# Last batch: residual prepared ahead, output in two halves, one state product on VectorE, and a new order of all steps

## The reference

```python
xn = layernorm(x)
s  = attention(xn)                    # q k^T / 128, own token masked, softmax, times v
g  = silu(top-2-of-8 experts(xn))     # 128 -> 256 -> 128, every expert is computed
x  = x + s * g
xn = layernorm(x)
s  = mamba(xn)                        # rms norm, in-projection, conv, scan, out-projection, + xn
g  = silu(top-1-of-8 experts(xn))     # 128 -> 512 -> 128, tokens sorted to their expert
x  = x + s * g
```

## Time and profile before

| | us |
|---|---|
| median of three runs | 978.26 |
| lowest, highest | 975.25, 983.37 |
| the profiled execution | 977.57 |
| its span, first to last instruction | 975.8 |
| busy: PE, DVE, ACT, POOL | 854.6, 777.3, 632.0, 592.7 |

### The profile page before, as it was taken

One profiled execution on the slowest core, in us unless ns is written; L12 is line 12 of the kernel. 1 busy time (PEld: TensorE's weight loads), 2 busy tenths in 40 slices (PEclk: granted clock), 3 DMA queues, 4 the chain that ended last, 5 costly groups with the idle time before them and its releaser, 6 DMA issues.

```text
span 975.8 us, 15806 instructions
## 1 busy us (share of the span) xinstructions
PE 854.6 (88%) x4624; PEld 583.0 (60%) x4624; DVE 777.3 (80%) x1479; ACT 632.0 (65%) x1379; POOL 592.7 (61%) x556
## 2 busy tenths in 40 slices
PE   5987898999799978999799979999799967785995
PEld 2773475775467746775567746775567735552662
DVE  3234537899988998799888998799888998877995
ACT  3524735868577775878477766878487765665661
POOL 0010202758856595858866694858766696869675
PEclk9987799999999998999899998999899997877999
DMA  7200103223322432224212332224213332333451
GB/s 265 88 1 13 33 12 98 85 76 123 99 71 75 109 120 85 84 87 132 95 55 87 107 120 75 84 88 133 93 57 106 95 109 98 117 99 95 134 146 52
DMA packets 79429, 90.28 MB, mean 93 GB/s; under 512 B 8450, under 2 KB 49906, under 8 KB 78834
## 3 DMA queue, kind: packets, MB, share of 16 engines
q1 hardware_dynamic: 77298, 85.07, 27.9%
q0 software_dynamic: 2048, 4.20, 1.5%
HBM read 52.96 MB, written 13.04 MB: 68 GB/s over the span
## 4 chain that ended last, share of the span: by engine, by line
PE 53%; POOL 17%; DVE 15%; issue 10%; ACT 4%; SPq 1%; DMA 0%; DVEq 0%; POOLq 0%
PE work L825 9%; PE work L831 7%; POOL st L1474 7%; PE work L856 7%; DVE st L1304 6%; PE work L866 5%; PE yacc L890 5%; POOL y L1481 4%; PE work L754 3%; PE work L775 3%; POOL fe L1461 3%; POOL du L1435 2%; PE work L745 2%; PE work L798 2%; ACT prob L946 1%
## 5 line engine op out<-in xcount | busy, mean ns | idle before, releaser
L1474 POOL TENSOR_TENSOR st<-st,Cs 128x512 f32<-128x512 f32 x249 | 315.9, 1281 | 184.4 <-DVE st L1304 182.2
L946 ACT ACTIVATE dA<-delta,Aneg 128x512 f32<-128x512 f32 x256 | 176.0, 722 | 9.6 <-DVE st L1304 9.1
L1304 DVE TENSOR_TENSOR_SCAN st<-dA,dbu 128x512 f32<-128x512 f32 x128 | 154.8, 1210 | 13.4 <-ACT dA L946 9.2
L890 PE MATMUL yacc<-st,w_ident 128*128 128x512 f32 x256 | 141.3, 637 | 27.2 <-POOL st L1474 27.2
L1304 DVE TENSOR_TENSOR_SCAN st<-dA,b_row 128x512 f32<-128x512 f32 x123 | 148.7, 1209 | 2.9 <-DVE acc L1194 1.5
L831 PEld LDWEIGHTS work<-w_w2a,hid 128*128 128x128 f32 x1024 | 121.5, 192 | 27.6 <-issue 13.0
L825 PE MATMUL work<-xnT,w_w1a 128*128 128x512 f32 x256 | 130.4, 600 | 5.9 <-ACT ys L946 3.8
L1481 POOL TENSOR_TENSOR y<-y,st 128x512 f32<-128x512 f32 x105 | 133.4, 1271 | 2.9
L946 ACT ACTIVATE hsT<-work,hs 128x128 f32<-128x128 f32 x352 | 100.6, 373 | 49.5 <-PE work L856 49.5
L831 PE MATMUL work<-w_w2a,hid 128*128 128x128 f32 x1024 | 124.9, 276 | 7.6 <-DVE delta L1278 7.6
L856 PE MATMUL work<-xsT,hs 128*128 128x128 f32 x704 | 106.6, 303 | 19.1 <-ACT xsT L946 17.9
(11 more groups left out here) (190 smaller groups left out, 1308.3 us busy)
## 6 DMA issues: line engine op xcount, KB each, us to landing
Cs<-c_dram SPq DMA_DIRECT2D x128, 256.0 KB, 3.6
hs<-w_w1f SPq DMA_DIRECT2D x88, 258.0 KB, 2.4
xs_in<-xs_dram SPq DMA_DIRECT2D x16, 256.0 KB, 2.8
ys_dram<-ys SPq DMA_DIRECT2D x16, 256.0 KB, 3.9
w_w1f<-in_w1f_dram SPq DMA_DIRECT2D x1, 2064.0 KB, 8.1
x_in<-in_x_dram SPq DMA_DIRECT2D x8, 256.0 KB, 3.3
w_w2f<-in_w2f_dram SPq DMA_DIRECT2D x1, 2048.0 KB, 12.4
kept_dram<-x_tok SPq DMA_DIRECT2D x8, 256.0 KB, 4.5
```

The lines of the kernel that those rows point to most:

```text
L890: mm(yacc[:], ident[:], state(s), start=False, stop=(n == NS - 1)).then_inc(sig["y_sum0"], 1)
L946: return nc.scalar.activation(out, in_, func, **k)
L1304: V.tensor_tensor_scan(state(s), dA[:, s % DECAYS], (dbu0, rows_bank(n, b))[h][:], 0.0, ALU.mult, ALU.add).then_inc(sig["scan"], 1)
L1474: G.tensor_tensor(state(s), state(s), Cs[:, b.of(NS, n) % C_BUFS], ALU.mult).then_inc(sig["P"], 1)
```

## The change

All values are computed as before. In the last batch:

- `xr` becomes `0.5 * xn * g + xr` before the out-projection is there: POOL makes `y1 = xn * g`, DVE the rest.
- The out-projection goes into two banks, the first two tiles of 128 tokens into one and the last two into the other, with a signal after each. DVE turns each half into the output with two instructions of half the size, and SP stores each half by itself.
- The C product of step 31 is on DVE behind the last scan and not on POOL.

The places, shifts and banks of nearly all steps are new numbers, in all batches. The core of the diff:

```diff
-                elif g == "C" and name == "out":
+                elif g == "C" and name == "out" and b.is_(NB - 1):
+                    for k in range(2):
+                        sp.wait_ge(sig["ot"], b.of(1, k + 1))
+                        sp.dma_start(out[b.n, 256 * k:256 * k + 256].rearrange("(i p) d -> p i d", p=128), ot[:, 2 * k:2 * k + 2]
+                                     ).then_inc(sig["out"], 16)
...
-                pe.wait_ge(sig["P"], b.of(STEPS, s + 1))
+                if n == NS - 1:
+                    pe.wait_ge(sig["P_last"], 1)
+                else:
+                    pe.wait_ge(sig["P"], b.of(STEPS, s + 1))
                 mm(work[SPARE][:], ident[:], state(s), start=(n == 0), stop=(n == NS - 1)).then_inc(sig["y_sum1"], 1)
...
                 for t in range(NT):
+                    if b.is_(NB - 1) and t == NT // 2:
+                        last.then_inc(ready[g], 1)
+                        w = other_bank(b)
...
+            def last_times_c(s, b):
+
+                r = b.of(NS, NS - 1)
+                dve.wait_ge(c_ld[r % C_BUFS], 16 * (r // C_BUFS + 1))
+                dve.wait_ge(sig["scan"], b.of(STEPS, s + 1))
+                V.tensor_tensor(state(s), state(s), Cs[:, r % C_BUFS], ALU.mult).then_inc(sig["P_last"], 1)
...
                     if b.is_(NB - 1):
-                        dve.wait_ge(sig["xr"], b.of(16, 16))
-                        V.tensor_tensor(ot[:], ot[:], xr[:], ALU.add).then_inc(sig["ot"], 1)
-                    dve.sem_inc(free_of("C", step, b), 1)
+                        dve.wait_ge(sig["rest"], 1)
+                        V.scalar_tensor_tensor(xr[:], y1t, 0.5, xr[:], ALU.mult, ALU.add).then_inc(sig["opx"], 1)
+                        for k in range(2):
+                            half = slice(2 * k, 2 * k + 2)
+                            dve.wait_ge(ready["C"], READY["C", step, b.n] + k)
+                            r = tiles((bank("C", step, b), other_bank(b))[k][:])[:, half]
+                            V.scalar_tensor_tensor(r, r, 0.5, g1[:, half], ALU.mult, ALU.mult).then_inc(sig["s1"], 1)
+                            dve.wait_ge(sig["opx"], b.of(1, 1))
+                            dve.wait_ge(sig["s1"], b.of(1, k + 1))
+                            V.tensor_tensor(ot[:, half], r, xr[:, half], ALU.add).then_inc(sig["ot"], 1)
...
+                elif g == "C" and name == "op" and b.is_(NB - 1):
+                    pool.wait_ge(sig["g1"], b.of(1, 1))
+                    pool.wait_ge(sig["xr"], b.of(16, 16))
+                    G.tensor_tensor(y1t, xn1_tok[:, b.n % 2], g1[:], ALU.mult).then_inc(sig["rest"], 1)
...
-    ("P", "pe", 0, -1.09268, 7, -2, -3, None),
+    ("P", "pe", 0, -1.00164, 7, 4, 2, None),
```

More of the change, by code:

```diff
@@ L325 @@
     ("A", 0): (
[4 rows of a table removed]
[4 rows of a table added]
     ),
     ("H", 0): (
-        -1.11411, -1.06978, -1.05742, -0.89565, -0.90279, -0.83828, -0.88733, -0.81603, -0.81528, -0.80089, -0.79422, -0.57863,
-        -0.79157, -0.74780, -0.77419, -0.79303, -0.73709, -0.72833, -0.62595, -0.89555, -0.69538, -0.77574, -0.66455, -0.53536,
-        -0.45046, -0.49154, -0.77058, -0.61446,
+        -1.06926, -1.11488, -1.07138, -0.90278, -1.02776, -0.90721, -0.93188, -0.88885, -0.88768, -0.83181, -0.80060, -0.62522,
+        -0.80029, -0.78513, -0.77066, -0.79205, -0.74524, -0.73956, -0.65961, -0.27137, -0.69281, -0.78227, -0.77960, -0.61707,
+        -0.61469, -0.77950, -0.70521, -0.74534,
     ),
     ("A", 1): (
[4 rows of a table removed]
[4 rows of a table added]
     ),
@@ L530, in build @@
         y1 = sb("y1", [128, T])
+        y1t = y1[:].rearrange("p (i d) -> p i d", i=NT)
         dA = sb("dA", [128, DECAYS, T])
@@ L595, in bank, with other_bank @@
             return work[bank_of(g, step, b.n)]
+        def other_bank(b):
+            return work[1 - bank_of("C", ("op", 0), b.n)]
         def free_of(g, step, b):
@@ L700, in _ @@
                 do(g, step, Batch(n))
-            sp.wait_ge(sig["out"], 16 * NB)
+            sp.wait_ge(sig["out"], 16 * NB + 16)
         @block.tensor
@@ L903, in project @@
                 bank_free(pe, g, step, b)
+                if b.is_(NB - 1):
+                    last = LAST_IN[1 - bank_of(g, step, b.n)]
+                    emptied(pe, *last[:2], Batch(last[2]))
                 pe.wait_ge(sig["yo"], b.of(1, 1))
+                w = bank(g, step, b)
                 for t in range(NT):
+                    if b.is_(NB - 1) and t == NT // 2:
+                        last.then_inc(ready[g], 1)
+                        w = other_bank(b)
                     for h in range(NH):
-                        last = mm(bank(g, step, b)[:, t * 128:(t + 1) * 128], du[:, par, h, t * 128:(t + 1) * 128],
+                        last = mm(w[:, t * 128:(t + 1) * 128], du[:, par, h, t * 128:(t + 1) * 128],
                                   W["woutT"][:, h * 128:(h + 1) * 128], start=(h == 0), stop=(h == NH - 1))
@@ L1319, in c_step @@
                 elif step[0] == "op":
-                    filled(dve, "C", step, b)
                     since(dve, sig["out"], b.of(16))
-                    r = tiles(bank("C", step, b)[:])
-                    V.tensor_tensor(r, r, xn1_tok[:, par], ALU.add).then_inc(sig["opx"], 1)
-                    dve.wait_ge(sig["opx"], b.of(1, 1))
                     dve.wait_ge(sig["g1"], b.of(1, 1))
-                    V.scalar_tensor_tensor(ot[:], r, 0.5, g1[:], ALU.mult, ALU.mult).then_inc(sig["s1"], 1)
-                    dve.wait_ge(sig["s1"], b.of(1, 1))
                     if b.is_(NB - 1):
-                        dve.wait_ge(sig["xr"], b.of(16, 16))
-                        V.tensor_tensor(ot[:], ot[:], xr[:], ALU.add).then_inc(sig["ot"], 1)
-                    dve.sem_inc(free_of("C", step, b), 1)
+                        dve.wait_ge(sig["rest"], 1)
[8 more added lines that the diff above has]
+                            V.tensor_tensor(ot[:, half], r, xr[:, half], ALU.add).then_inc(sig["ot"], 1)
+                    else:
+                        filled(dve, "C", step, b)
+                        r = tiles(bank("C", step, b)[:])
+                        V.tensor_tensor(r, r, xn1_tok[:, par], ALU.add).then_inc(sig["opx"], 1)
+                        dve.wait_ge(sig["opx"], b.of(1, 1))
+                        V.scalar_tensor_tensor(ot[:], r, 0.5, g1[:], ALU.mult, ALU.mult).then_inc(sig["s1"], 1)
+                        dve.wait_ge(sig["s1"], b.of(1, 1))
+                        dve.sem_inc(free_of("C", step, b), 1)
             def do(g, step, b):
@@ L1344, in do @@
                     scan(i, b)
+                    if b.is_(NB - 1) and i == STEPS - 1:
+                        last_times_c(i, b)
                 elif g == "C":
@@ L1490, in do @@
                     f_step(step, b)
-                elif g == "S" and name == "p":
+                elif g == "S" and name == "p" and not (b.is_(NB - 1) and i == STEPS - 1):
                     times_c(i, b)
@@ L1494, in do @@
                     add_state(i, b)
-                elif g == "C" and name == "op" and not b.is_(NB - 1):
+                elif g == "C" and name == "op" and b.is_(NB - 1):
+                    pool.wait_ge(sig["g1"], b.of(1, 1))
+                    pool.wait_ge(sig["xr"], b.of(16, 16))
+                    G.tensor_tensor(y1t, xn1_tok[:, b.n % 2], g1[:], ALU.mult).then_inc(sig["rest"], 1)
+                elif g == "C" and name == "op":
                     pool.wait_ge(sig["s1"], b.of(1, 1))
```

## The result

The changed kernel takes 983.18 us (median of 22 runs, 979.22 to 988.53), the kernel before 978.72 (22 runs beside it, 974.86 to 983.75). The ratio is 1.0051, with a 95% interval of 1.003 to 1.0072: slower by half a per cent. Forecast were 979.5, a range of 967 to 989, and 0.74 for "within 1%"; the measured median is 3.7 above the first. The profiled execution took 980.58, its span is 978.8 against 975.8. What follows counts span: 3.0 us are to be explained by it.

A forecast was written before the change was run, and what follows sets the result against it. Bound: a ring per period, POOL's queue from `pos` to `ft`, then PE's from h0 to `rk`. Terms +10.3 - 1.2 - 8.7 + 0.8 = +1.2 on 977.57 gave 978.8, or 979.5 by median; range 967 to 989.

The forecast's parts named there:

- Start, +10.3 -1.2: Start: beta products ahead of H.z0 cost 10.3 us; y0 and b1 moved out of PE's later full stretch give 1.2.
- The rival that they run at full clock: Start: beta products stay at full clock and take 7.0 us, z0 is 5.3 later, total 974.5; chance 0.15.
- Periods, -8.7: All periods: `ft` sooner gives 1.35 us in each of five, 1.9 in the sixth; bounds 0 and -16.
- the clock: 0.4: Behind each period's stall: PE's slow-clock stretch shrinks somewhat, giving 0.4 us a period.
- a clock of 1.00 behind the stall: Period's end: a granted clock of 1.00 behind PE's stall would show the forecast wrong.
- The period without A: Sixth period, where DVE leads: 1.4 us from DVE's wait for PE and 0.5 from its wait ahead of H.bc.
- worth only what DVE waits for PE there: Period without A: the sixth stall's gain is limited to DVE's wait of 1.48 us for PE, taken as 1.4.
- Tail, +0.8: Behind the last scan: C.y starts later and the residual chain takes 4.4 us; 0.8 us slower, bounds -0.6 and +1.8.
- The DVE product of step 31 lies in 5.67 us of idle time: Tail: DVE's product of step 31 costs nothing, at worst 0.7 us for a POOL step that it holds up.
- The start decides, slower: Start: all 64 products, z0 and x1T at half clock, +13.7 us; periods give only 0.95 each; total 984.3; chance 0.25.
- The periods win: Periods: the slow stretch shrinks by half or more, each period gives 2.9 us, total 971.1; chance 0.2.
- The tail does what its name says: Tail: the rest of the residual is made during the scans; gives 0.6 us, total 978.1; chance 0.05.

The follow-up runs named there:

- e1: The changed kernel with the beta products back in their old place, ahead of H.hT on PE: 973.04 us, ratio 0.9923 to the kernel before.
- e2: The kernel before with the beta products alone moved behind H.xi0 on PE: 993.91 us, ratio 1.0154 to the kernel before.
- e3: The changed kernel with `ft` late again, behind two other steps in POOL's queue: 999.92 us, ratio 1.0223 to the kernel before.
- e4: The kernel before with `ft` alone moved ahead of two other steps in POOL's queue: 976.58 us, ratio 0.9979 to the kernel before.
- e5: The changed kernel with the last batch's scan 31 written to PSUM, where DVE's C product reads it: 985.24 us in one execution.
- e6: The changed kernel with the last batch's `g` made ahead of C.y on DVE: 986.48 us in one execution.
- e8: The changed kernel with the edits of e1, e5 and e6, and a15 ahead of e15 on PE: 969.87 us, ratio 0.9924 to the kernel before.
- e10: The same program as e8, run a second time beside e9: 967.88 us, ratio 0.9908 to the kernel before.
- e9: The code of e8 with the order tables of e7: 969.47 us, ratio 0.9917 to the kernel before.
- e15: Not a run: a step of the kernel with work on PE and POOL, which DVE's C.y needs; no time of its own as a run.
- e7: e4 with y0 also moved ahead of a0 in PE's queue: 973.13 us, ratio 0.9938 to the kernel before.

## Why the prediction was right, and where not

The time lies in the range and within 1%, as forecast. By span the sum was +1.2 and +3.0 came. The terms were off by more, in both directions: the start 2.7 us dearer, the tail 1.7 dearer, the periods and the last scans 2.6 cheaper. That they nearly cancel is luck. (Of the rivals' times, 971.1 and 984.3 stand on the scale of the profiled execution and 974.5 and 978.1 on that of the median, 0.7 higher. "No gain in the periods" adds up to 991 and not 990.)

**Start, +10.3 -1.2.** The mechanism is as forecast: e1 and e2 each show it with one number moved. The size was too small: the products took 13.65 us, the upper bound of the forecast (13.5), where I took 12.0 for "a short spell at full". There was none: PE had idled 12.58 us before hT, hT and xi0 ran at half clock, and the clock stayed there. With z0's own 1.05 us more, that makes 12.8 of the 12.6 us. The row that I leaned on was the wrong neighbour: in the old place PE came into the products out of full work, at 1.00, in the new one out of rest, at 0.50. The first interval gave back 0.8 of the 1.2. That this comes from y0 and b1 is not shown: e2, which moves nothing there, gave back 1.45. The rival that they run at full clock, 0.15, fell: the rows have 0.50 while PE is busy 3.40 of 3.40 us. The rule of the Trainium skill, "TensorE: Matmul & The Clock Gate", Part 1, that the clock follows busy time, would have given 7.0 us; the windows disagree, and the measurement decides.

**Periods, -8.7.** Measured: -11.2 in the five, +0.4 in the sixth. `ft` sooner and ACT late next was the right reading: -2.3 from `pos` to h0 where 1.95 was forecast, ACT's F.silu with no idle time before it, and e3 and e4 show it with this one step moved. The mis-sized term is the clock: 0.4 was taken, with a bound of 3 if the spell went. From h0 to `pos` the steps moved in (0.8) and the wait for the copy (0.2) were to cost 1.0, less 0.4 for the clock; measured is 0.05 a period. So the clock, if all of it is the clock, gave 0.95. The trace of the kernel before bears this out: its h0 with 3.4 us of half clock takes 72.2 us to the next `pos`, the other four 73.4 on the mean. Had all five been like the first, they would sum to 361.0 us. The changed kernel has 366.0, 1.0 more a period, which is what the steps and the copy were to cost; and the kernel before has 365.8, so its clock cost 0.95 a period. The reason that I gave for a small term, PE's idle time bunching even more ahead of h0, was wrong in the trace: it lies in pieces of 1.19, 0.89 and 1.45 us with PE's steps between them. But the pieces don't settle the length of the half clock either. It is 3.4 and 6.8 us behind the same 2.8 in the kernel before, and 0 and 3.4 behind the same 1.3 to 1.5 in the changed kernel. What decides it stays open. One of the forecast's signs of being wrong, a clock of 1.00 behind the stall, is there in two periods of five, and another, a new wait of over half a us on PE that repeats, is the 0.76 above.

The -11.2 is also the good end of what this order does. From the second `pos` to the last scan it gains 11.3 us on the kernel before in its own trace, and 6.9, 9.2, 9.3, 8.2 and 12.0 in those of e1, e5, e6, e8 and e10, which have the same order there (but for a15 in the last two): 9.5 on the mean of the six. For that the forecast had 8.7.

The period without A was to give 1.9 and took 0.4. The 1.48 and 2.08 us of the earlier trace rows are gone, and DVE has new waits in their stead. Two of 0.42 and 0.41 us are for ACT, at 836.08 and 837.71; the other two in its timeline in the changed kernel:

```profile
852.53 0.19 DVE L1157 TENSOR_REDUCE am<-work 128x4 f32<-128x32 f32 x1 [1.06 <-PE work L790]
856.24 1.22 DVE L1323 TENSOR_TENSOR_SCAN st<-dA,dbu 128x512 f32<-128x512 f32 x1 [1.70 <-PE yacc L899]
```

Their sum is 3.6 us, what the old ones held. In this trace the step that fails is "worth only what DVE waits for PE there": a wait taken away in a queue that is moved as a whole is not yet time won. But in e1, e5 and e10, with the same order, the wait of 1.70 is 0.6 or less, and the period takes 92.8, 92.1 and 92.9 us for the 94.6 before: 1.7 to 2.4 less, as forecast. So the failure is this execution's, and the order does not force it.

**Tail, +0.8.** Measured +2.5, 2.1 to the last sum and 0.4 for the store. The 0.4 is not shown to be the split's: from the last sum to the end it is 2.6 us before, and with the store split it is 3.0 here and in e3 but 2.2 in e6, e8, e9 and e10. That half the size gives 0 isn't shown either: in the changed kernel's trace stores of 256 KB land after 2.6 us and those of 128 KB after 1.8 (medians), where the kernel before had 3.1 for 256 KB and for 32. The failing step is "The DVE product of step 31 lies in 5.67 us of idle time: nothing, and at worst 0.7". It took 5.17 us, and e15 then waited 0.42 for it at half clock. C.y's middle instruction starts 8.49 us after the last scan, 6.53 before: +1.96 where 0.75 was forecast. e5 takes the block away and leaves the 14.4 us, so the block is not the sole cause: PE's last four steps at half clock take as long. The clock alone is not the cause either: in e3, which keeps block and order, it is back at full 4.3 us behind the last scan, as early as before, and C.y's middle instruction still starts 8.15 us after that scan, 1.6 later than before. The longer half clock adds 0.3 to that here. With `g` ahead, the product from PSUM and a15 ahead of e15 (e8) 2.5 us go. e6 gives `g` 1.5 of them; how the rest divides between a15 and the product, no run tells apart. The chain behind C.y was right, 4.50 us for 4.4 forecast.

**The rivals.** "The start decides, slower" had 984.3 and named half clock for all 64 products, which is what happened; its other half, a period that gives only 0.95, did not. "The periods win" had the spell that shrinks by half, which happened as well. "The tail does what its name says" fell by e6. The number came out near the first of them because gains in the periods ran against it, as far as the second has them: not its 2.9 us a period, but 2.2.

## What to carry to other kernels

Filler work belongs where an engine has nothing to do, and a queue's order is to be read for what it uncovers: 64 tiny products, free in one gap, cost 10 to 15 us behind the next step. Before a stall is shortened, look at what its late engine's next step will wait for (e4 gave 1.8 us, one more move 3.4). A product moved to an idle VectorE beside a busy GpSimd was short here only with one of its inputs in PSUM. And one trace each is not enough: the same order gained 6.9 to 12.0 us in six of them.

## What the runs showed of the hardware

**VectorE behind GpSimd.** A tensor product on DVE with both inputs in SBUF took 5.17 us in the changed kernel and again in e1, e3 and e6, 0.69 with one input in PSUM (e5, e8). It began 0.3 us after POOL's first product and ended 0.56 us after POOL's fourth instruction in a row. A hint was in the trace of the kernel before, at 805.56: C.y's middle instruction, two inputs in SBUF, begins 0.07 us after a single product of POOL, takes 1.75 us and ends 0.56 after it. In the six other periods it takes 0.76. The Trainium skill, "SBUF — State Buffer", section "Who interferes with whom", has a VectorE instruction with two SBUF inputs contend with GpSimd's reads for a shared port, so that the one that comes second waits for the other's whole instruction. The trace agrees that it waits, but it waited for four instructions, not for one.

**The start varies, and so do the periods.** With the same order at the start, the first `pos` came at 109.9, 109.6, 112.8 and 116.8 us (changed kernel, e3, e5, e6), with the beta products back at 103.0, 95.5 and 100.3 (e1, e8, e10), and with the old order at 97.3, 97.3, 99.8 and 99.7 (before, e4, e7, e9). Windows of 80 to 95 us in e8 and e10, columns as in the earlier trace rows:

```profile
80.00:95.00 15.00, 9.77 (x48) 5.27 (x48) 8.43 (x25) 7.72 (x15) 0.00 (x0) 0.93 0.00 1
```
```profile
80.00:95.00 15.00, 13.54 (x32) 7.46 (x33) 5.68 (x14) 5.47 (x11) 0.00 (x0) 0.57 0.00 1
```

e8 and e10 are one program: 0.93 granted in the one execution and 0.57 in the other, and 4.9 us between their starts. In e6, with the latest start, it is 0.50. Behind the start the periods of the new order are 106.4 to 106.8 us in the changed kernel, but in e1, e5, e6, e8 and e10 one or two of the five take 107.4 to 108.3. So single spans are compared here mark by mark, and the price of the start is told by the medians of e1 and e2.
